# Two narrow attentions that normalise their own input, a shorter launch, and shares spread in bf16 parts

## The reference, cut to what matters

```
x = x + attn(layernorm(x)); x = x + xattn(layernorm(x), ctx); x = x + ffn(layernorm(x))
```

```
attn = softmax(sum_d(q*k) * 64**-0.5, over the heads)
state = decay*state + (1-decay)*attn[..., None]*v
out = q*state + sigmoid(q*aug), then @ Wo + bo, then a layernorm
```

## Time and profile before

| | us |
|---|---|
| median of 3 runs | 1717.16 (1716.86 to 1717.72) |
| profiled execution, its own time | 1709.27 |
| its span in the trace | 1707.2 |
| PE busy | 1489.2 (87% of the span) |
| DVE busy | 1163.2 (68%) |
| ACT busy | 900.7 (53%) |
| POOL busy | 714.1 (42%) |

### The profile page before, as it was taken

The page is one execution under the profiler, slowest core; times in us unless marked ns, Lnnn a source line. Parts: engine busy times, 40 slices in busy tenths (PEclk is TensorE's granted clock), DMA queues, the critical chain, the costliest instruction groups (busy, mean ns, idle before and its releaser), DMA issues. The chain is left out here.

```text
span 1707.2 us, 28841 instructions
## 1 busy us (share of the span) xinstructions
PE 1489.2 (87%) x9987; PEld 959.8 (56%) x9987; DVE 1163.2 (68%) x2480; ACT 900.7 (53%) x2612; POOL 714.1 (42%) x677
## 2 busy tenths in 40 slices
PE   4999785869889999888899888999986886879998
PEld 2665544545567775553343335888864443557776
DVE  4898574369867775555898897777767886644443
ACT  2675342247677772225776764777752443444443
POOL 2556351032455441414898895333351244431000
PEclk9999995989999999988999999999997998989999
DMA  7000000000000000020000000000000000000000
GB/s 289 1 2 1 1 2 1 0 1 2 2 1 2 2 2 1 1 89 0 1 1 0 1 1 1 2 2 2 1 1 1 1 1 0 1 1 7 7 7 7
DMA packets 3165, 18.95 MB, mean 11 GB/s; under 512 B 592, under 2 KB 720, under 8 KB 2256
## 3 DMA queue, kind: packets, MB, share of 16 engines
q1 hardware_dynamic: 3024, 17.14, 2.5%
HBM read 16.09 MB, written 1.05 MB: 10 GB/s over the span
## 5 line engine op out<-in xcount | busy, mean ns | idle before, releaser
L827 POOL TENSOR_TENSOR l_xattn_probs<-l_xattn_probs,l_xattn_recip 128x512 f32<-128x512 f32 x128 | 133.1, 1040 | 223.2 <-DVE l_xattn_recip L766 222.7
L999 ACT ACTIVATE l_attn_probs<-ps,l_attn_neg_max 128x128 f32<-128x128 f32 x512 | 144.7, 383 | 76.8 <-DVE l_attn_neg_max L1048 76.8
L2547 POOL TENSOR_TENSOR l_mamba_hc<-l_mamba_h,l_mamba_c 128x512 f32<-128x512 f32 x128 | 158.9, 1267 | 0.0
L2449 DVE TENSOR_TENSOR_SCAN l_mamba_h<-ps,l_mamba_dBx 128x512 f32<-128x512 f32 x128 | 152.5, 1211 | 1.8 <-ACT ps L2346 0.7
L2219 PE MATMUL ps<-l_mamba_hc,w_const 128*128 128x512 f32 x256 | 136.6, 637 | 19.4 <-POOL l_mamba_hc L2547 16.5
L3212 DVE SCALAR_TENSOR_TENSOR xn<-ps,l_gates,xn 128x128 f32<-128x128 f32 x224 | 63.1, 344 | 116.8 <-PE ps L2857 116.6
L761 DVE COPY l_xattn_probsT<-ps 128x512 f32<-128x512 f32 x128 | 87.9, 687 | 71.5 <-PE ps L613 71.5
L2992 ACT ACTIVATE wkv<-ps,w_early 128x512 f32<-128x512 f32 x112 | 70.7, 683 | 114.5 <-PE ps L2846 114.4
L2857 PEld LDWEIGHTS ps<-w_early,wkv 128*128 128x128 f32 x896 | 109.0, 194 | 28.6 <-issue 18.7
L2857 PE MATMUL ps<-w_early,wkv 128*128 128x128 f32 x896 | 111.1, 277 | 8.8 <-ACT wkv L2992 8.8
L712 ACT ACTIVATE l_xattn_probs<-ps,l_xattn_neg_max 128x128 f32<-128x128 f32 x256 | 91.7, 389 | 41.5 <-DVE l_xattn_neg_max L756 41.5
(11 more groups left out here) (524 smaller groups left out, 3630.3 us busy)
## 6 DMA issues: line engine op xcount, KB each, us to landing
w_early<-in_l_moe SPq DMA_DIRECT2D x1, 3669.0 KB, 12.1
w_l_xattn<-in_l_xattn SPq DMA_DIRECT2D x1, 2176.0 KB, 22.6
w_early<-in_l_xattn SPq DMA_DIRECT2D x1, 1890.0 KB, 14.6
w_l_attn<-in_l_attn SPq DMA_DIRECT2D x1, 1242.0 KB, 25.1
ctx<-in_ctx SPq DMA_DIRECT2D x1, 1088.0 KB, 10.5
x<-in_x SPq DMA_DIRECT2D x2, 512.0 KB, 4.2
ctxT<-in_ctxT SPq DMA_DIRECT2D x1, 1024.0 KB, 8.4
out_x<-x SPq DMA_DIRECT2D x4, 256.0 KB, 2.9
```

Of the source, the lines that this page charges most:

```text
L827: nc.gpsimd.tensor_tensor(probs[:, D % 2, n, :, :], probs[:, D % 2, n, :, :], along(recip[:, D % 2, n, :], [P, HALF, P]), ALU.mult).then_i ...
L999: ins = nc.scalar.activation(probs[:, t % 4, g, :], S_of(t)[:, g * P:(g + 1) * P], ACT.Exp, bias=neg_max[:, t % 2, g:g + 1], accum_out=total)
L2449: nc.vector.tensor_tensor_scan(flat(h[:, t % 2, half, :, :]), G.ps[:, DA_BANK[half], :], flat(dBx[:, t % 2, half, :, :]), 0.0, ALU.mult, A ...
L2547: nc.gpsimd.tensor_tensor(heads4(hc[:, t % 4, half, :]), h[:, t % 2, half, :, :], c_sb[:, t % 3, :, :], ALU.mult).then_inc((hc0_set, hc1_s ...
```

## The change

1. The first block issues only `x`, the constants and layer 0's attention weights, with the constants between the halves of `x`. While they land, DVE takes the statistics of all sequences and the variances of the first eight, POOL their powers. The other 12 transfers (`load_rest`) are issued by SP in the first attention's block.
2. Both narrow attentions lose their `layernorm` block and use `Lead`. The normals, transposes and copies stand in the attention's own streams, quads 2 and 3 between steps 0 and 1. Small constants and the layer 1 query scale move into the block as well.
3. Layer 1's attention gets products of two constants on PE (`keep_clock`), 10 before step 0 and 5 in each of steps 0 to 3, into a bank that nobody reads.
4. In layer 3's attention DVE splits the shares into three bf16 parts whose sum is the f32 value; one bf16 product transposes the three parts, and one bf16 product spreads and adds them (`sel_e` stacked three times, cast to bf16 by POOL at the block's start).

```diff
+def keep_clock(nc, G, bank, n):
+    for _ in range(n):
+        nc.tensor.matmul(G.ps[:, bank, :], G.ident_bf[:], G.mask_kq_bf[:].unsqueeze(1).broadcast_to([P, 4, P]), start=True, stop=True)
...
@@ narrow_attention
+        O_BANK, X_BANK = 6, 7
+        lead = Lead(nc, G, s, tag, (4, 5, O_BANK, O_BANK))
+        @block.sync
+        def _(sp):
+            if first:
+                load_rest(nc, G, sp)
+            lead.sync(sp)
         @block.tensor
             def project(b):
+                lead.wait(pe, b)
...
+            pe.wait_ge(G.loaded["const"], 16)
+            lead.needs(pe)
+            lead.tensor(pe, 0)
             if projected:
                 project(0)
+                pe.wait_ge(consts, 1)
                 pe.wait_ge(p_taken, 1)
-            else:
-                pe.wait_ge(masked, 2)
+            lead.tensor(pe, 1)
+            if not projected:
+                keep_clock(nc, G, X_BANK, 10)
             for t in range(STEPS + OUT_LAG + 1):
                 if t < STEPS:
                     scores(t)
+                if not projected and t < OUT_LAG:
+                    keep_clock(nc, G, X_BANK, 5)
                 if projected and s_ == 0 and b + 1 < NB:
                     project(b + 1)
+                if t < 2:
+                    lead.tensor(pe, 2 + t)
                 if T_LAG <= t < STEPS + T_LAG:
+                    if t == T_LAG:
+                        lead.wait(pe, QUAD)
                     turn(t - T_LAG)
                 if V_LAG <= t < STEPS + V_LAG:
+                    if t == V_LAG:
+                        lead.wait(pe, NB - 1)
                     times_v(t - V_LAG)
...
@@ its scalar stream
+            lead.scalar(act, 0)
             if projected:
                 act.wait_ge(masked, 2)
                 take(0)
+            lead.scalar(act, 1)
...
+                if t < 2:
+                    lead.scalar(act, 2 + t)
...
@@ its vector stream
+            lead.rest.early(dve, nc.vector, 0, 0)
+            dve.wait_ge(G.loaded["const"], 16)
+            if first:
+                small_constants(nc, G, dve).then_inc(consts, 1)
+            if prepare:
+                lead.needs(dve)
+                prepare(dve)
             (head mask, clearing of v, ones)
+            lead.rest.variances(dve)
+            for q in range(1, lead.rest.first // QUAD):
+                lead.rest.early(dve, nc.vector, 0, q)
+            lead.rest.late(dve, nc.vector, 0)
...
@@ its gpsimd stream
+            lead.rest.early(pool, nc.gpsimd, 1)
             pool.wait_ge(masked, 2 if projected else 3)
-            keys(0)
+            if projected:
+                lead.rest.scales(pool)
+                lead.rest.late(pool, nc.gpsimd, 1)
+                keys(0)
+            else:
+                keys(0)
+                lead.rest.scales(pool)
+                lead.rest.late(pool, nc.gpsimd, 1)
...
@@ l0_attn, l1_attn
-    layernorm(nc, G, "l0_attn", "l0_attn")
-        layernorm(nc, G, "l1_attn", "l1_attn", also=prepare)
...
@@ l2_ffn_and_l3
-                    mm = nc.tensor.transpose(G.ps[0:H, T_BANK, j * P:(j + 1) * P], probs[:, j, :], G.c["ident"])
+                    mm = nc.tensor.matmul(G.ps[0:3 * H, T_BANK, j * P:(j + 1) * P], probs3[:, j, :, :].rearrange("p n h -> p (n h)"),
+                                          G.ident_bf[:], start=True, stop=True)
...
-                    nc.tensor.matmul(G.ps[:, P_BANK[c % 2], :], sel_e[:, c * P:(c + 1) * P], probsT[:],
+                    nc.tensor.matmul(G.ps[:, P_BANK[c % 2], :], spread3[:, c * P:(c + 1) * P], probsT[:],
...
-                nc.scalar.copy(probsT[0:H, :], G.ps[0:H, T_BANK, :]).then_inc(p_copied, 1)
+                nc.scalar.copy(probsT[0:3 * H, :], G.ps[0:3 * H, T_BANK, :]).then_inc(p_copied, 1)
...
-                dve.wait_ge(blank, 2)
+                dve.wait_ge(blank, 3)
...
-                nc.vector.tensor_tensor(probs[:], probs[:], along(top[:], [P, QUAD, H]), ALU.mult).then_inc(p_set, 1)
+                link(nc.vector.tensor_tensor(probs[:], probs[:], along(top[:], [P, QUAD, H]), ALU.mult))
+                for n in range(2):
+                    link(nc.vector.tensor_copy(probs3[:, :, n, :], probs[:]))
+                    link(nc.vector.tensor_tensor(probs[:], probs[:], probs3[:, :, n, :], ALU.subtract))
+                nc.vector.tensor_copy(probs3[:, :, 2, :], probs[:]).then_inc(p_set, 1)
...
+            nc.gpsimd.tensor_copy(spread3[:], full(G, "const", "sel_e")).then_inc(blank, 1)
...
@@ load(nc, G, aps, with_stats): SP issues x half 0, const, x half 1, l0_attn; then
+    @G.first.vector
+    def _(dve):
+        for b in range(NB):
+            if b % (NB // 2) == 0:
+                dve.wait_ge(G.loaded[f"x{b // (NB // 2)}"], 16)
+            if b == begun.first:
+                begun.variances(dve)
+            begun.stats(b)
+        dve.wait_ge(begun.seen, NB)
+    @G.first.gpsimd
+    def _(pool):
+        nc.gpsimd.memset(G.neg_half[:], -0.5).then_inc(exponent, 1)
+        pool.wait_ge(exponent, 1)
+        begun.scales(pool)
+def load_rest(nc, G, sp):
+    (issues ctxT, ctx1 and the other groups but l3_moe, in the former order)
```

More of the change, by code:

```diff
@@ L36 @@
     "const": dict(ident=(128, 128), mask_qk=(128, 128), mask_kq=(128, 128), decay=(128, 128),
-                  heads=(128, 16), heads16=(128, 8), sel_e=(8, 512), low=(128, 84), rows3=(128, 32), pair16=(128, 2)),
+                  heads=(128, 16), heads16=(128, 8), sel_e=(24, 512), low=(128, 84), rows3=(128, 32), pair16=(128, 2)),
     "l0_attn": dict(wq=(128, 128), wk=(128, 128), wv=(128, 128), wo=(128, 512)),
@@ L838, in _, with narrow_attention @@
                     ahead.apply(pool, nc.gpsimd, 3)
-def narrow_attention(nc, G, tag, w=None, q_scale=None):
+def narrow_attention(nc, G, tag, w=None, q_scale=None, prepare=None):
     H, DH, U, VP = 16, 8, 2, 32
@@ L851, in narrow_attention @@
     OUT_LAG = V_LAG + (2 if projected else 1)
+    first, G.started = not G.started, True
     with Scope(nc, G, tag) as s:
@@ L866, in narrow_attention @@
         (masked, p_made, p_taken, q_set, v_set, k_ready, scored, maxed, exped, row_summed, row_inverted, evened, turned, copied, summed,
-         o_copied, o_turned, inverted, normed, out_made, added) = (s.sem(n) for n in (
+         o_copied, o_turned, inverted, normed, out_made, added, consts) = (s.sem(n) for n in (
              "masked", "p_made", "p_taken", "q_set", "v_set", "k_ready", "scored", "maxed", "exped", "row_summed", "row_inverted",
-             "evened", "turned", "copied", "summed", "o_copied", "o_turned", "inverted", "normed", "out_made", "added"))
+             "evened", "turned", "copied", "summed", "o_copied", "o_turned", "inverted", "normed", "out_made", "added",
+             "consts"))
+        O_BANK, X_BANK = 6, 7
+        lead = Lead(nc, G, s, tag, (4, 5, O_BANK, O_BANK))
         ahead = Ahead(nc, G, s, twice=not projected)
         DONE = OUT_LAG + U * ahead.first
-        O_BANK, X_BANK = 6, 7
         Q, K, V, E = (slice(n * P, (n + 1) * P) for n in range(4))
@@ L1074, in keys @@
                 else:
+                    lead.wait(pool, b)
                     source = G.xnT[:, b, :]
@@ L1117, in prepare @@
             nc.vector.scalar_tensor_tensor(q_scale[:], w["rot"], 8 ** -0.5, w["ent"], ALU.mult, ALU.mult).then_inc(own, 1)
-        layernorm(nc, G, "l1_attn", "l1_attn", also=prepare)
-        narrow_attention(nc, G, "l1_attn", q_scale=q_scale[:])
+            dve.wait_ge(own, 1)
+        narrow_attention(nc, G, "l1_attn", q_scale=q_scale[:], prepare=prepare)
 class Wkv:
@@ L2616, in l2_ffn_and_l3 @@
         probs = s.sb("probs", [P, QUAD, H])
-        probsT = s.sb("probsT", [P, QT])
-        sel_e = full(G, "const", "sel_e")
+        probs3 = s.sb("probs3", [P, QUAD, 3, H], BF16)
+        probsT = s.sb("probsT", [P, QT], BF16)
+        spread3 = s.sb("spread3", [P, QT], BF16)
         v_sb = s.sb("v", [P, 2, QT])
@@ L3415, in _, with load @@
             received_normals(LAST)
-def load(nc, G, aps):
+def load(nc, G, aps, with_stats):
+    s = Scope(nc, G, "load")
+    begun = Ahead(nc, G, s, first=NB // 2) if with_stats else None
+    exponent = s.sem("exponent")
     @G.first.sync
@@ L3428, in _ @@
               .then_inc(G.loaded[f"x{n}"], 16)
-        for group in LAYOUT:
-            if group == "l3_moe":
-                continue
+            group = ("const", "l0_attn")[n]
             sp.dma_start(G.pack[group], aps[group]).then_inc(G.loaded[group], 16)
-            if group == "l0_attn":
-                sp.dma_start(G.ctxT[:], aps["ctxT"]).then_inc(G.loaded["ctxT"], 16)
-                sp.dma_start(G.ctx1, aps["ctx1"]).then_inc(G.loaded["ctx1"], 16)
+    if not with_stats:
+        return
+    @G.first.vector
[13 more added lines that the diff above has]
+def load_rest(nc, G, sp):
+    for group in LAYOUT:
+        if group == "l0_mlstm":
+            sp.dma_start(G.ctxT[:], G.aps["ctxT"]).then_inc(G.loaded["ctxT"], 16)
```

(9 more changed lines are left out.)

## The result

On one chip, in alternation, the changed kernel took 1695.63 us (median of 4 runs, 1689.38 to 1702.74) against 1717.01 (4 runs, 1715.46 to 1717.72): ratio 0.9878, 95% interval 0.9835 to 0.9921. The profiled execution took 1689.38 us.

A forecast was written before the change was run, and what follows sets the result against it. PE is busiest, but the edited places were read as timelines, with waits, PE's clock and DVE as limits. Terms -6.6 - 4.9 - 0.3 = -11.8 us took 1717.16 to 1705.4; range 1699.5 to 1711.

The forecast's parts named there:

- I carry the difference over: Whole kernel: the profiled execution's 7.9 us below the median of the runs stay, so 1717.16 - 11.8 = 1705.4.
- term 2: Layer 1's attention: one meeting goes and constant products keep PE at 2.4 GHz; -4.9 us, bounds -3 to -6.5.
- Blocks run one after another, hence a us saved between two meetings of the engines is a us of the span: Whole kernel: the ground for costing the three edited places as timelines; a us saved there counts fully.
- Term 1: Launch and layer 0's attention: keys ready 7.9 us earlier, 1.35 us come back; -6.6 us, -10.6 at best.
- Rival A: Layer 0: the clock rises at the same moment after launch as before; +1.6 us, 1707.0; chance 0.12.
- Rival B: Layer 1: constant products don't hold the clock, step 4 6.9 us later than before; total 1717.2, chance 0.10.
- Term 3: Layer 3's shares: bf16 products replace f32, five more DVE operations per quad; -0.3 us, bounds -3 to +4.4.
- rival D: Layer 3's attention: PE is busier less, so the clock falls to 1.2 GHz; a whole quad costs 27: 1732; chance 0.05.
- Rival C: Layer 3's shares: the edit only adds DVE time, all on the path; +4.4 for -0.3, 1710.1; chance 0.07.

The follow-up runs named there:

- e13: The kernel before, unedited, profiled a third time, on a fourth chip: 1717.29 us.
- e1: The changed kernel again with no edit, on the first chip: 1695.51 us in this execution, median 1695.48 us of 6 runs, ratio 0.9899 to the kernel before.

## Why the prediction was wrong

Means over all profiles of each form, us:

| stretch | old form | new form | difference |
|---|---|---|---|
| launch to first attention's end (`x` order as in the change) | 171.9 (8: 170.1 to 174.2) | 164.5 (7: 162.2 to 165.5) | -7.4 |
| mLSTM, by the launch in front | 92.3 (8) | 89.9 (10) | -2.4 |
| layer 1 attention | 122.8 (8: 119.9 to 125.6) | 115.6 (8: 114.8 to 119.4) | -7.2 |
| last block, by the shares | 435.1 (11: 433.1 to 437.0) | 436.4 (6: 435.7 to 437.0) | +1.3 |

Their sum is -15.7, where the medians gave -21.4, -18.2 and -18.6 in the three comparisons. The half-width of the ratios' intervals is 5.0 to 7.4 us, so the rest of 2.5 to 5.7 is not resolved; mamba (without its normalising block) with layer 2's cross attention, 511.8 in the mean of the kernels with the old launch and 511.7 with the new, doesn't hold it. The profiles may hold too many short executions: the five of the kernel before average 1710.4 us, below each of the four medians of its runs (1711.4 to 1718.3). By these means the forecast of -11.8 lacks 3.9 us: -2.4 in mLSTM, which it put at nothing, -2.3 in layer 1, -0.8 in the launch, and +1.6 in the last block against them. That alone would still end inside the range.

**The step that failed: "I carry the difference over".** The profiled execution lay 7.9 us under the median, and I assumed those 7.9 in parts that the change leaves alone. They lay mostly in parts that it edits. The profile of 1717.29 us (e13), which is at the median, has layer 1 at 125.6 for 119.9, the last block at 437.0 for 433.6, mLSTM at 93.5 for 91.3 and the first stretch at 171.6 for 174.2. Layer 1's old form takes one of two lengths, and the rows I costed it from the earlier trace rows were of the short kind. PE's scores in that profile, of the long kind, change level at 376.55, in step 5 (normalising block from 348.3, attention from 353.5), in the short one at step 4:

```profile
371.63 2.08 PE L904 MATMUL ps<-l_attn_k_one,l_attn_q 32*128 32x512 f32 x4
376.55 1.18 PE L904 MATMUL ps<-l_attn_k_one,l_attn_q 32*128 32x512 f32 x4
```

An edit that pins the clock removes that spread as well, so it is worth more against the median than against a lucky profile: -7.2 over all profiles for -4.9, beyond term 2's bound of -6.5. Two executions at the medians show the whole of it, e13 at 1717.29 and e1 at 1695.51, with every block not named here equal within 0.2: first stretch -7.3, mLSTM -3.8, layer 1 -10.6, last block -0.4, together 22.0 of span. I picked them by their times, and they ran on two chips, so they illustrate the account and don't prove it.

**A second step failed: "Blocks run one after another, hence a us saved between two meetings of the engines is a us of the span".** It put every block whose code stays at nothing, without a reason. mLSTM gave 2.4 us in the means.

**Term 1.** -7.9 at step 0's scores was -6.64: the second half of `x` cost 1.3 us where I allowed "a few tenths" and 0.45 for the meeting. Of the 1.35 to be paid back 1.0 was (step 2: -5.64). Then the clock: -9.64 at step 5, in the profile pair. Over all profiles the stretch gives -7.4 for -6.6 forecast, inside its bound.

**Rival A** falls in its form (the rise at one wall moment, 51): the rise came at 20 to 39 us behind the new launch and 32 to 51 behind the old one, in both with falls in between in some profiles. What it cited, the Trainium skill, TensorE: Matmul & The Clock Gate, Part 1, that the moment isn't tied to the kernel's start and differs from run to run, is what these traces show: in the three profiles of the changed kernel the scores change level at 27, 34 and 39 us.

**Term 2.** -4.9 at step 4 was forecast; the block's start to step 4 took 17.5 us for 18.05. Two errors cancel, which is luck: the first ten products ran at the lower level, 4.01 us for 2.2 (3.8 to 4.0 in six of the eight profiles of the new form, 2.3 in the other two), so step 0 came 4.92 us behind the start for 3.95; and the later steps were shorter than I walked them. **Rival B** is out: the level held in eight of nine profiles, and without the products it didn't rise for five steps.

**Term 3.** Quad 0: -0.5 for -0.55; DVE's five operations are 0.18 to 0.19 us each, 0.22 apart, as costed, but for one subtraction in quad 3 that takes 1.14 us beside a POOL operation, in all seven profiles with bf16 shares. The prediction holds four of the five open to that; this one of twenty was held. Quad 1's first fed product is 3.7 us later than before; from quad 0 on that is +4.2 for +1.1. From there to quad 2 it is -0.8, as forecast. With the products repeated it is +0.9, so the missing 3.1 us come back (2.8 at quad 1, 0.5 of quad 0's gain going with them): they are **rival D's** mechanism, at a tenth of its price. I held against D that "the level was held at that density". Busy time doesn't tell the two apart, 7.31 and 7.74 us in the first two windows of 10 us where the level falls, 8.59 and 6.58 with products repeated, where it doesn't; what the chip goes by stays open. I priced D by halving PE for a quad; in fact some 10 us ran at the lower level (0.17 of 30 us, doubled) and partly under DVE, which bounds that stretch. Over all profiles the term is +1.3 for -0.3, since the block is long without bf16 shares too in six of eleven. **Rival C** is out as an account: 0.9 of quad 1's delay is DVE's time.

**The untouched mLSTM.** It gave 2.4 us that no step had. In the first pair of profiles, DVE's `floor_row` and POOL's `q_pair` start within 0.02 us of each other; before, and after:

```profile
189.11 1.89 POOL L2066 TENSOR_TENSOR l_mlstm_q_pair<-xnT,w_const 128x1024 f32<-128x1024 f32 x1
189.13 2.01 DVE L1978 TENSOR_TENSOR l_mlstm_floor_row<-l_mlstm_cs,l_mlstm_neg_m 128x128 f32<-128x128 f32 x1
```

```profile
179.57 0.29 DVE L2032 TENSOR_TENSOR l_mlstm_floor_row<-l_mlstm_cs,l_mlstm_neg_m 128x128 f32<-128x128 f32 x1
179.59 2.03 POOL L2120 TENSOR_TENSOR l_mlstm_q_pair<-xnT,w_const 128x1024 f32<-128x1024 f32 x1
```

Whichever comes second waits: a DVE operation with two SBUF inputs takes 0.29 us ahead of POOL's and 1.80 to 2.01 behind it. It came second in all eight profiles with the old launch (in four of them 0.02 to 0.04 us behind POOL's operation, in the other four some 0.3 us) and in one of ten with the new. That is the lock that the Trainium skill, SBUF — State Buffer, section Who interferes with whom, describes. The block takes 89.6 to 89.7 us where DVE is first and 91.3 to 91.8 where it is second; three profiles with the old launch show 93.0 to 93.8, with a granted clock of 0.80 to 0.84 at 20 to 30 us behind its start, for 1.00. Why the new launch shifts this meeting stays open.

The version with f32 shares and `x` first has a median 5.0 us below the changed kernel's on the one chip where both ran, and 16.6 and 23.6 below the kernel before on its two.

## What to carry to other kernels

A product that is taken off PE isn't always free: here the clock fell behind the edit and came back with the products repeated. Look at the granted clock there, not only at the busy time. Where PE must wait a few us ahead of a dense stretch, products of constants can keep or bring the higher level for when the work comes: in layer 1 they did in eight of nine profiles, in layer 0, ahead of lighter work, they gained nothing. And before a profile is costed, look whether its stages are typical: of five profiles of the kernel before, three show layer 1 at 120 and two at 126, and the first two taken were both short.

## What the runs showed of the hardware

- Unchanged blocks take one of a few lengths, not a spread: mamba 275.3, 277.5 or 281.0, layer 2's cross attention 229.0 or 233.4, with 275.3 and 229.0 together in all three of their executions. The granted clock tells the short ones: around the end of mamba, 280 to 300 us behind its normalising block's start, a window of 10 us shows 0.66 to 0.85 in the seven longer ones that I read and 1.00 in the three short ones. What starts either is open.
- The level can fall again while the steps go on: in layer 0 with six products ahead it rose at 20 us, was down within step 2 (27.2) and back at 42.5.
- Layer 1 lost some 3 us in its last two steps in just those profiles where its early steps had been long: four of eight in the old form, and in the new one the profile without products and the one where they failed. What links the two isn't known.
- Which of two engines came first decided over 1.5 us or more of wait: by 0.04 us of shift in the first pair of profiles, and on the same side in 17 of 18.
